# A fused Mamba scan, attention and MLP kernel on Trainium2: side work of the scan's steps spread over more steps, some steps of the front moved

## The reference

```python
# first half: a Mamba block with 16 states per channel, D_INNER = 2048
xz = layernorm(x) @ in_proj_w.T ; x_ssm, z = split(xz)
xc = silu(causal_conv4(x_ssm) + conv_b)
dt_r, B, C = split(xc @ x_proj_w.T)            # 1, 16, 16 columns
dt = softplus(dt_r @ dt_proj_w.T + dt_proj_b)
h_t = exp(dt_t * A) * h_(t-1) + dt_t * B_t * xc_t   # per channel and state
y = sum_n h_t[n] * C_t[n] + D * xc
x = x + layernorm((y * silu(z)) @ out_proj_w.T)
# second half: attention with gated value and output experts, then an MLP
s = layernorm(x)
q, k = rope(s Wq), rope(s Wk) ; v = gated expert values
s = layernorm(s + expert_output(softmax(q k / 8) v))
x = x + layernorm(layernorm(s + relu(s W1 + b1) W2 + b2))
```

## Time and profile before

| | us |
|---|---|
| median of 3 runs (range) | 3783.7 (3778.4 to 3904.4) |
| profiled execution, device time | 3785.1 |
| its span, slowest core (5) | 3783.5 |
| spans of the 8 cores | 3764.1 to 3783.5 |
| first scan to last scan, core 5 | 243.4 to 1692.1 |

### The profile page before, as it was taken

One profiled execution on the slowest core, in us unless ns is written; L12 is line 12 of the kernel. 1 busy time (PEld: TensorE's weight loads), 2 busy tenths in 40 slices (PEclk: granted clock), 3 DMA queues, 4 the chain that ended last, 5 costly groups with the idle time before them and its releaser, 6 DMA issues.

```text
span 3783.5 us, 59592 instructions; the slowest of 8 cores (3764.1 to 3783.5 us)
## 1 busy us (share of the span) xinstructions
PE 3139.9 (83%) x16992; PEld 1441.0 (38%) x16992; DVE 2382.0 (63%) x2765; ACT 2134.0 (56%) x3136; POOL 1305.0 (34%) x799
## 2 busy tenths in 40 slices
PE   4777666768676776776699999999979999999997
PEld 2333333334333333332244444444424444344443
DVE  6779998998899899976565444444414444412333
ACT  4578786777777777764366666666630000133432
POOL 1339997878887877770000000000000000000000
PEclk9877888889898989888899999999989999999998
DMA  6422225322432334215365675423071010611111
GB/s 156 60 36 46 42 43 112 120 91 66 100 119 86 70 99 136 91 42 151 57 85 83 97 101 80 75 39 83 12 197 34 23 40 17 206 56 51 62 62 45
DMA packets 152118, 300.01 MB, mean 79 GB/s; under 512 B 16986, under 2 KB 64730, under 8 KB 149756
## 3 DMA queue, kind: packets, MB, share of 16 engines
q1 hardware_dynamic: 127408, 228.03, 21.0%
q0 software_dynamic: 24240, 67.91, 12.9%
q10 hardware_dynamic: 156, 0.27, 0.0%
HBM read 324.39 MB, written 77.40 MB: 106 GB/s over the span
## 4 chain that ended last, share of the span: by engine, by line
PE 59%; DVE 15%; issue 10%; ACT 10%; DMA 3%; SPq 1%; POOL 1%; DVEq 0%; ACTq 0%; POOLq 0%
PE psAcc L1767 12%; PE psV L1555 12%; DVE mid L764 10%; PE psH L1936 6%; PE psS L1569 6%; PE psP L1584 5%; ACT mid L793 5%; PE psH L1951 5%; PE psXZ L474 2%; PE psO L365 2%; PE psXZ L566 2%; PE psXZ L810 2%; SPq L196 1%; PE psY L826 1%; ACT L793 1%
## 5 line engine op out<-in xcount | busy, mean ns | idle before, releaser
L764 DVE TENSOR_TENSOR_SCAN mid<-mid,hcol,psXZ 128x512 f16<-128x512 f32 x1024 | 1223.3, 1258 | 147.9 <-PE psXZ L810 67.5
L856 POOL TENSOR_TENSOR mid<-mid,cb_sb 128x1024 f16<-128x1024 f16 x512 | 1082.2, 2123 | 258.1 <-DVE mid L764 223.2
L793 ACT ACTIVATE mid<-mid,c_pk 128x512 f32<-128x512 f32 x1024 | 699.1, 716 | 132.4 <-DVE mid L764 128.6
L810 PE MATMUL psXZ<-dgall,uT 128*128 128x128 bf16 x4096 | 415.0, 231 | 410.1 <-DVE mid L764 390.0
L1635 ACT ACTIVATE attT<-psS 128x1024 bf16<-128x1024 f32 x512 | 522.3, 1024 | 261.6 <-PE psS L1569 257.2
L810 PEld LDWEIGHTS psXZ<-dgall,uT 128*128 128x128 bf16 x4096 | 286.4, 102 | 741.7 <-issue 689.5
L1555 PE MATMUL psV<-wvA,act_a 128*128 128x512 bf16 x2048 | 524.0, 380 | 20.3 <-DVE vgt L1652 20.3
L1652 DVE TENSOR_TENSOR vgt<-psV,gv_tm 128x512 bf16<-128x512 f32 x256 | 176.8, 691 | 403.0 <-PE psV L1555 403.0
L826 PE MATMUL psY<-mid,c_id 128*128 128x512 f16 x1024 | 335.4, 412 | 7.7 <-POOL mid L856 7.6
L196 POOL DMA_DIRECT2D wvA<-wv x16 | 14.6, 910 | 895.9 <-PE psV L1555 643.3
L1569 PE MATMUL psS<-qT_aug,kT_aug 65*128 65x512 bf16 x1024 | 306.4, 380 | 6.1 <-ACT attT L1635 5.1
(11 more groups left out here) (216 smaller groups left out, 3882.1 us busy)
## 6 DMA issues: line engine op xcount, KB each, us to landing
woD<-woutb SPq DMA_DIRECT2D x192, 256.0 KB, 2.7
wzD<-wzb SPq DMA_DIRECT2D x64, 256.0 KB, 2.8
wvA<-wv POOLq DMA_DIRECT2D x16, 1024.0 KB, 14.2
wob<-wo POOLq DMA_DIRECT2D x16, 1024.0 KB, 29.1
woD<-wqkb SPq DMA_DIRECT2D x48, 256.0 KB, 2.6
cb_sb<-xp_d SPq DMA_DIRECT2D x32, 256.0 KB, 10.4
w1b<-w POOLq DMA_DIRECT2D x8, 1024.0 KB, 29.1
w2b<-w POOLq DMA_DIRECT2D x8, 1024.0 KB, 26.8
```

Of the source, the lines that this page charges most:

```text
L764: inc(v.tensor_tensor_scan(h_band[:, (g % NH) * TW:(g % NH + 1) * TW], daD[g % NDA][:], psX[:, (g % NX) * TW:(g % NX + 1) * TW], hcol[:, c ...
L793: inc(s.activation(daD[g % NDA][:], dtD[di % 2][:], AF.Exp, scale=c_A[:, dc * NN + n: dc * NN + n + 1]), "da")
L810: last = t.matmul(psX[:, o:o + 128], uT[di % 2][:, sb * 128:(sb + 1) * 128], diagB[(tc * 4 + sb) % 8][:, n * 128:(n + 1) * 128], start=Tru ...
L856: inc(gp.tensor_tensor(hcD[p % NHC][:], h_band[:, s0 * TW:(s0 + 2) * TW], cb_sb[:, (p % 8) * 2 * TW:(p % 8 + 1) * 2 * TW], op=OP.mult), "hp")
```

## The change

It moves pieces to other steps, splits some over more steps, and changes three places of the front.

- `z_pe` is cut in four: two matmuls in each of the steps n = 1 to 4, as an entry of `ops` (so behind the other work of its step on PE). `silu_act` moves from n = 5 to 6, `ut_pe` from 11 to 12, `ut_act` from 14 to 15, `T` and `Te` from 7 and 9 to 8 and 10.
- The token tiles are 36 steps apart, `op` k at base + (3k)//2 instead of base + 2k. From the last `op` (base + 22, before 30): `lnA` 2 steps later (before 3), `xrm` 6 steps after `lnA` (before 1), `lnC` 2 after `xrm`, `lnD` 1 after that, `src` 6 after `lnD` (before 2).
- The Q/K units start at step 174 and are 5 apart: two matmuls in each of four steps, `qke` 6 steps after the first.
- SP's loads and stores for the norms shift with them.
- Front: `ddA` lies in `xc_a` (channel tiles 13 to 15), and the wait for its store moves from ACT's `xs` and DVE's `cv` of unit 0 to ACT's `si` of unit 13. `dg0` becomes 4 DVE instructions of 128 x 2048 that read the identity and B by broadcast access patterns, and the copy to `bTF` goes. `xc`, `bt`, `be`, `dg0` move one unit later. `xp` lags by 3 units up to unit 19 and by 4 after that.

```diff
-    ddA = mid[:, 2048:2048 + DC * 384]
+    ddA = xc_a[:, 13 * S:16 * S]
...
-        if h == 0:
-            s.copy(bTF[:], psTF[h][:, 0:64])
...
-        base = (i // 4 + 1) * DC * NN + 40 * (i % 4) + 16
+        base = (i // 4 + 1) * DC * NN + 36 * (i % 4) + 16
         for k in range(16):
-            ops.setdefault(base + 2 * k, []).append(("op", i, k))
-        for nm, at in [("lnA", 33), ("xrm", 34), ("lnC", 36), ("lnD", 37), ("src", 39)]:
+            ops.setdefault(base + (3 * k) // 2, []).append(("op", i, k))
+        for nm, at in [("lnA", 24), ("xrm", 30), ("lnC", 32), ("lnD", 33), ("src", 39)]:
             ops.setdefault(base + at, []).append((nm, i, 0))
-        gt = base + 43 + (7 - (base + 43)) % NN
+        gt = base + 41 + (8 - (base + 41)) % NN
...
-            g = (c + 1) * DC * NN + 188 + 4 * m
-            ops.setdefault(g, []).append(("qk", c * 16 + m, 0))
-            ops.setdefault(g + 1, []).append(("qk", c * 16 + m, 1))
-            ops.setdefault(g + 3, []).append(("qke", c * 16 + m, 0))
+            g = (c + 1) * DC * NN + 174 + 5 * m
+            for j in range(4):
+                ops.setdefault(g + j, []).append(("qk", c * 16 + m, j))
+            ops.setdefault(g + 6, []).append(("qke", c * 16 + m, 0))
+    for di in range(TC * DC):
+        for j in range(4):
+            ops.setdefault(di * NN + 1 + j, []).append(("z", di, j))
...
-    def z_pe(t, di):
-        wge(t, "ute", di + 1)
-        wge(t, f"wz{di % 2}", 16 * (di // 2 + 1))
-        for k in range(8):
+    def z_pe(t, di, j):
+        if j == 0:
+            wge(t, "ute", di + 1)
+            wge(t, f"wz{di % 2}", 16 * (di // 2 + 1))
+        for k in range(2 * j, 2 * j + 2):
             last = t.matmul(psZ[:], wzD[di % 2][:, k * 128:(k + 1) * 128],
                             ln0T(k)[:, chunk(di)], start=(k == 0), stop=(k == 7))
-        inc(last, "zt")
+        if j == 3:
+            inc(last, "zt")
...
-             18: [("xc", 0)], 19: [("bt", 0)], 20: [("be", 0)], 21: [("dg0",)],
+             19: [("xc", 0)], 20: [("bt", 0)], 21: [("be", 0)], 22: [("dg0",)],
...
-        if u >= 2:
-            order += [("xp", u - 2)]
-    order += [("xp", 30), ("ut0",), ("si", 31), ("xp", 31), ("ute0",)]
+        lag = 3 if u < 20 else 4
+        if u >= lag and u != 20:
+            order += [("xp", u - lag)]
+    order += [("xp", 28), ("xp", 29), ("xp", 30), ("ut0",), ("si", 31), ("xp", 31), ("ute0",)]
...
-                if u == 0:
-                    wge(s, "ddw", 16)
...
+                if u == 13:
+                    wge(s, "ddw", 16)
                 inc(s.activation(xc_tile(m)[:, hcols(h)], caF[u % 2], AF.Silu), "si")
...
-                for n in range(NN):
-                    for sb in range(4):
-                        last = v.tensor_scalar(diagB[sb][:, n * 128:(n + 1) * 128], c_id[:],
-                                               bTF[:, sb * 16 + n:sb * 16 + n + 1], None,
-                                               op0=OP.mult)
+                for sb in range(4):
+                    idb = bass.AP(c_id[:].tensor, c_id[:].offset,
+                                  [c_id[:].ap[0], [0, NN], [1, 128]])
+                    bcol = bass.AP(c_bT[:].tensor, c_bT[:].offset + sb * 16,
+                                   [c_bT[:].ap[0], [1, NN], [0, 128]])
+                    last = v.tensor_tensor(diagB[sb].rearrange("p (n c) -> p n c", n=NN),
+                                           idb, bcol, op=OP.mult)
...
-            if n == 5:
+            if n == 6:
                 silu_act(s, di)
-            if n == 14 and di + 1 < NDI:
+            if n == 15 and di + 1 < NDI:
                 ut_act(s, di + 1)
...
-                if n == 1:
-                    z_pe(t, di)
-                if n == 11 and di + 1 < NDI:
+                if n == 12 and di + 1 < NDI:
                     ut_pe(t, di + 1)
```

More of the change, by code:

```diff
@@ L274, in _build @@
     rF = sbd("rF", [128, 16], F32)
-    bTF = sbd("bTF", [128, 64], F32)
     psTF = [psY[i][:].bitcast(BF16) for i in range(2)]
@@ L314, in _build @@
         for m in range(16):
-            g = (c + 1) * DC * NN + 188 + 4 * m
-            ops.setdefault(g, []).append(("qk", c * 16 + m, 0))
-            ops.setdefault(g + 1, []).append(("qk", c * 16 + m, 1))
-            ops.setdefault(g + 3, []).append(("qke", c * 16 + m, 0))
+            g = (c + 1) * DC * NN + 174 + 5 * m
[5 more added lines that the diff above has]
+            ops.setdefault(di * NN + 1 + j, []).append(("z", di, j))
     for g, nm in [(2, "xc"), (5, "bt"), (6, "be")]:
         ops.setdefault(g, []).append((nm, 1, 0))
-    PE_OPS = ("op", "T", "qk", "bt")
+    PE_OPS = ("op", "T", "qk", "bt", "z")
     ACT_OPS = ("xrm", "src", "Te", "qke", "xc", "be")
@@ L331, in op_pe @@
             bt_pe(t, i)
+        elif nm == "z":
+            z_pe(t, i, k)
         elif nm == "op":
@@ L355, in op_pe @@
         else:
-            c, m, hf, x = i // 16, i % 16, k, wqx(i)
-            if hf == 0:
+            c, m, x = i // 16, i % 16, wqx(i)
+            if k == 0:
                 wge(t, WOS[x % NWO], 16 * (x // NWO + 1))
@@ L363, in op_pe @@
                     wge(t, "qe", i - 1)
-            for j in range(4 * hf, 4 * hf + 4):
+            for j in range(2 * k, 2 * k + 2):
                 last = t.matmul(psO[:, (m % 2) * 512:(m % 2 + 1) * 512],
@@ L368, in op_pe @@
                                 start=(j == 0), stop=(j == 7))
-            if hf == 1:
+            if k == 3:
                 inc(last, "wu")
@@ L461, in ut_pe @@
             nte = sum(1 for g, l in ops.items() for nm, _, _ in l
-                      if nm == "Te" and g < (di - 1) * NN + 11)
+                      if nm == "Te" and g < (di - 1) * NN + 12)
             wge(t, "te", nte)
@@ L696, in _ @@
                 if u == 0:
-                    wge(v, "ddw", 16)
                     v.memset(xsF[0][:, 0:3], 0.0)
@@ L940, in _ @@
             l0 = wat[wox(i, 15)]
-            at(l0 - 12, xr_ld, i)
-            at(l0 + 8, x1_st, i)
-            at(l0 + 11, src_st, i)
+            at(l0 - 14, xr_ld, i)
+            at(l0 + 12, x1_st, i)
+            at(l0 + 19, src_st, i)
         at(3 * 256 + 100, wr_ld, 0)
```

## The result

| | before | changed |
|---|---|---|
| median of the runs shown, us | 3844.0 (4) | 3815.7 (4) |
| executions with no slowed die, us | 3778.4, 3783.7 | 3733.9, 3739.1 |
| ratio, 95% interval | | 0.9881 (0.9853 to 0.9910) |
| profiled execution: span, core 5 | 3783.5 | 3737.6 |

Both medians hold executions in which one die ran at a lower granted clock (for the changed kernel 3892 and 4057 us), so all comparisons here go by the ratio, which leaves them out. The ratio is a gain of 1.2%, within 2%, as the forecast had it most likely. It forecast 3729 of 3783.7, a ratio of 0.9855, inside the interval. The median of 3815.7 lies outside the range of 3690 to 3770; 3733.9 and 3739.1 lie in it.

What follows compares the result with a forecast made beforehand. DVE was taken to bound the scan, with only its 148 us of idle to win. Front 15 plus scan 39 (chunk 0 2, the others 37) made 54 off the profiled 3785.1: 3731, forecast as 3729, range 3690 to 3770.

Steps and rivals of the forecast that it cites:

- chunk 1: Second chunk of the scan: of 46 us of DVE idle, with a surplus at its start, 14 us go.
- SP's order: SP's loads: new order costs nothing; a weight slot reloads in 3 us and comes up again after 6 steps, 7 us.
- silu's wait for z: Scan, n = 6: ACT's silu waits 0.2 us, 0.6 behind an op piece, 0.9 in Q/K blocks.
- Front: Before the scan: store wait, dg0 and later xp together give 15 us less, between 7 and 25.
- The store's wait: Front, unit 0: ACT no longer waits for the store; 11.2 us go there, 5 to 11 gained, taken as 11.
- The later xp: Front: the xp lag removes most of PE's waits for silu; gain between 0 and 8 us, taken as 2.5.
- Chunk 0: First chunk of the scan: an n = 2 gap of 1.1 us traded for 0.6 to 1.4 at n = 6; -10 to +8, taken -2.
- Chunks 2 and 3: Third and fourth chunks of the scan: DVE idle 26.5 us against 38, 11.5 less in each.
- A: Scan: no silu wait appears, or ACT's slack exceeds 2.3 us; time 3690 to 3705 us; chance 0.30.
- B: Scan: POOL or chunk starts take back DVE's gain in chunks 1 to 3, only the front wins; 3765 us; chance 0.12.
- C: Scan: spreading z leaves PE more at half clock, z and silu end late; slower, 3878 us; chance 0.05.
- D: Scan: the moves do not shift the waits at all, only the front gains; 3770 us; chance 0.08.

Runs made afterwards that it cites:

- silu at 7: The changed kernel with silu one step later, at n = 7 instead of 6, all else the same; ratio to the kernel before 0.9767.
- best: The changed kernel with silu at n = 7, src of tile 0 two steps later, xrm, lnC, lnD of tile 2 two earlier; ratios 0.9772 and 0.9744.
- front_only: The kernel before with the changed front alone, scan untouched; ratio 0.9949.
- scan_only: The changed kernel with the old front; ratio to the kernel before 0.9925.
- no_store_wait: The kernel before with only the skip matrices in another buffer and the wait for their store moved to unit 13; ratio 0.9967.
- qke_later: The kernel before with only the Q/K eviction two steps later, 5 steps after the first half of its matmuls instead of 3; ratio 0.9906.

## Why the prediction was right or wrong

The direction and the mechanism were right, and the sum was too high by a fifth. What failed are two of its terms: what chunk 1 gives, with the cost of SP's order that was put at nothing, and the length of silu's wait for z.

**What bounds the kernel: right.** DVE is the engine to feed, and only its 148 us of idle could go. 29 of them went; with silu at 7, 65; with `best`, 75.

**Front: right in its parts, the sum 4 us low.** Forecast 15, measured 19 by `front_only`. The store's wait was put at 11 (12), dg0 at 1.5 (1.6, and 2283 ns for one instruction against 2290 worked out). The Trainium skill's rule on steps (VectorE: DVE Perf Modes, "What auto-detection actually checks") agrees with this: all operands have 16 bits, B is read with step 0 along the row, and the 2048 elements took the time that the earlier trace rows give at 1.04 ns an element. No run has the same operands at step one beside it. The later xp was put at 2.5 and is the mis-sized term of the front, with 5 to 6 left for it by difference.

**Chunk 0: right in mechanism, 2.5 us off.** Forecast 2, measured 4.5 on core 5 (332.6 to 328.1 from its first to its last scan), -1.7 to 3.6 on the other seven. The n = 2 gap went and one at n = 6 came, 0.6 to 1.8 us. POOL leaves little room: in a window of the chunk it is busy 195.5 of 200 us now (192.7 before).

```profile
300.00:500.00 200.00, 135.38 (x931) 72.04 (x928) 190.81 (x168) 159.38 (x255) 195.47 (x128) 0.84 0.23 44
```

**Chunks 2 and 3: right in mechanism, 2 us short each.** Forecast 11.5 each, measured 9.2 and 10.2. DVE's idle in them is 28.9 and 28.3, where the prediction's sum has 26.5. The term that was too small is silu's wait for z: the text's 8 for 11 blocks and 0.9 for each of five Q/K blocks hold some 8 us of waiting a chunk, and the traces have 12.9 and 14.2. The wait of 0.2 without and 0.6 with an op piece in front was worked out from three rows. The block shown above has 0.62, but the mean over the first eleven blocks of the third chunk is 0.70, and 1.04 over its last five. The waits of xrm, src and qke went as said, and the bursts stand where they were put: 2.9 at n = 6 in block 7 (2.6 worked out), 1.7 at n = 7 in block 3 (1.95).

**Chunk 1: wrong, 14 forecast and 5.5 measured** (4.9 to 9.5 on the other cores). Two steps of the prediction failed here. The first is that the start of the chunk gives 2.5 us more than in the others: in its first two blocks DVE's idle did not shrink, it grew from 12.7 to 15.2. The second is "SP's new order costs nothing as I see it": a weight tile comes too late, and PE waits 3.76 us for it:

```profile
588.76 6.58 SPq L196 DMA_DIRECT2D woD<-woutb  x3
...
593.88 1.01 PE L346 MATMUL psO<-woD,xc_a 128*128 128x512 bf16 x2 [3.76 <-DMA woD<-woutb]
...
595.56 1.28 DVE L772 TENSOR_TENSOR_SCAN mid<-mid,hcol,psXZ 128x512 f16<-128x512 f32 x1 [1.47 <-PE psXZ L818]
```

The slow issues are not new. Before the change SP took as long for the C tiles at this place (9.03 us for three, in both kernels). What is new is that the op pieces come 1.5 steps apart instead of 2, so the cover of "6 steps, 7 us", set against a reload of 3 us from a quiet stretch, is not enough here. `tiles_only`, which has the new steps of the tiles and of their loads and stores, and nothing else, shows it:

```profile
PE psO L342 <- DMA woD<-woutb: 6.0, 4, 2.8
```

That wait stands on all eight cores of every kernel with the new tile steps (at the start of this chunk 1.8 to 3.8 us in the changed one), and on no core of the kernel before, `front_only`, `no_store_wait` or `qke_later`. Its price is smaller than the wait: DVE stands 1.47 us, then 0.85, behind it, 2.3 of the 8.5 that are missing. Gaps that POOL ends in the two blocks grew by about 1, and silu's wait for z is 16.8 us in this chunk, where the next has 12.9. The rest is not told apart by any run.

**The rivals.** A (silu does not wait) is refuted: 61 waits. But its price was the interesting part. I put those waits at some 25 us and their removal, with part of the bursts, at 25 to 40, and saw it as a kernel that might turn out this way by itself. They are 51.7, and one more step removes them, for 43. B (only the front wins) falls with `scan_only`; its 21.7 us a block should have been 22.0 by the prediction's own gain of 39. C (the clock) falls: the mean granted clock of core 5 is 0.932, it was 0.926, and over the scan alone it is 0.88, it was 0.87. D falls with the first waits.

**The sum.** 54 forecast from the profiled execution, 46 measured in the spans, 45 by the ratio. Chunk 1 is 8.5 short, chunks 2 and 3 together 4, and 4.4 went in the stretch behind the scan; the front gave 5 more on this core and chunk 0 some 3 more. That the total came within 9 us is in part luck: errors of both signs cancelled.

## What to carry to other kernels

When a consumer is moved later together with its producer, compare when the last piece is ready with when the consumer could start, both measured from the same event; spreading a producer over four steps moved its end by three steps, the consumer moved by one, and an otherwise good change lost half of its worth. And when several waits on one engine lie behind one another, the parts tried alone do not add: each alone may show nothing (z, 0.9997) or too much (Q/K, 36 us), so after removing a wait look at once for the next one on the same engine. A reload time read in a quiet stretch is no price for a stretch in which the queue reloads everything at once, and uses closer together eat the cover that hid it.

## What the runs showed that was not expected

- Silu moved by one step of 1.2 us gives 43 us in 64 blocks, all that its waits fell by (51.7 to 8.8), although POOL is nearly full in the first chunk. On core 5 the 7.8 us of waits in that chunk were worth 3, the 44 behind it 37.
- A table load of 1283 ns follows the exp before it within 0.02 us and the silu follows the load as closely, so the pair of loads costs 2 x 1.28 us here: from the first load to the next exp it is 3.20 us in all 64 blocks of the kernel before, 0.60 of it silu.
- An issue on SP takes 0.3 us in a quiet stretch and 2 to 3 us at the start of a chunk (3 in 6.58 us above), before the change as after it.
